# Four attention layers on one core: the second layer in steps of two units, the third layer's projections in halves

## The chip, the cores and the metric

The kernel runs on one core of a Trainium2 chip. The metric is the device time of one execution in microseconds. Before the change it is 1268.54 us, the median of three runs (1267.23 to 1269.7). The core has five engines that run beside one another, each in its own program order: PE (matrix multiply), DVE (vector), ACT (activations and copies), POOL (general) and SP (issues DMAs). They are synchronised by semaphores alone, so an instruction waits only for what its engine waits for just ahead of it.

## The reference, cut to what matters

Four layers follow one another on tokens x (4 batches of 256 tokens, 256 wide) with one context (4 x 256 x 256). The first is large (two cross attentions of 16 heads, 128 wide, and an MLP). The three others have small heads. The kernel calls them l = 1, 2, 3, and l = 1 and 2 are what the change touches:

```python
# l = 1 ("first small-head layer"): 16 heads, 16 wide, 256 context keys, mask, then an MLP
x = layer_norm(hidden, ln1_w, ln1_b)
q, k, v = x @ q_w + q_b, ctx @ k_w + k_b, ctx @ v_w + v_b
scores = where(mask, q k^T * scale, min);  out = softmax(scores) v
hidden = out @ cproj_w + cproj_b + residual
# l = 2 ("second"): queries from the latents y, keys from ctx and y together: 512 keys
h = concatenate([ctx, y], axis=1)
q, kv = y @ q_w + q_b, h @ kv_w + kv_b
attn = softmax(where(full_mask, q k^T / 16, -inf));  out = attn v @ out_w + out_b + residual
# l = 3: 32 heads, 8 wide, 8 key heads, full additive mask
```

All of it is float32. Exactness is kept by splitting operands in a high and a low part: a projection of one 128-row block is six matmuls of 256 columns (three products for each of two halves of the depth, `mm3`).

## The kernel before, in words

`class Heads` (line 1198) holds the plan of one small-head layer, and `heads_pe`, `heads_act`, `heads_dve`, `heads_pool` and `heads_sp` write it out for each engine. The work is a list of units. In layer 1 a unit is one head of one batch (64 units, 16 a batch), in layer 2 half of the queries of one head against 512 keys (128 units, 32 a batch). For each unit:

- `by_query` (L1975): scores with the queries as rows, into one of the `SB` banks; two matmuls of 256 columns (L1987) in layer 1, one of 512 (L1983) in layer 2. `maxima` on DVE reads the bank (L2233 or L2236) and so frees it.
- POOL splits the maxima of a group in high and low (L2274, L2276), PE transposes them (`turn_maxima`, L2079), ACT copies them (L2173) and POOL sends them by DMA as two more rows of the query tile Q (L2290).
- `by_key` (L1992): L steps later, the scores again with the keys as rows and the maximum and mask subtracted by the added rows (two matmuls, L2001), into one of the two `STB` banks, and ACT's exp (L2159) from there into `PT`.
- `attend` (L2056): values times `PT` for four heads at once (L2069) into bank `OB`, and ACT copies it (L2167).

A pair of units has y = 0 and y = 1: the first has its operands in partitions 0 to 63, the second in 64 to 127. The queries and the keys are 49 and 51 rows deep.

One pass of the loop `for n in range(s.steps())` is a step. WIDTH is the units of a step, LAG the steps from a unit's queries to its keys, TURN when the maxima are transposed, MEET when and in how many parts `attend` runs. Layer 1 has WIDTH 1, LAG 11, TURN 3, MEET (2, 2): a step is one unit of queries and one of keys (with the other y), written by `queries` and `keys`, and each attend is two parts in two steps. It has two `SB` banks; the transposed maxima have a bank of their own (`RB`). Layer 2 has WIDTH 2, LAG 5, TURN 1, MEET (1, 1), written by `fours`, and three `SB` banks, the third being `RB`; the maxima are transposed into the right half of `OB`.

What else is in the steps stands in tables by the step's number within a batch. IN_LAYER: the preparations for the next batch. These are the transposition of its tokens ("turn", bank PB), their high and low part ("th" on ACT, "tl" on DVE), the projections for queries, context keys, latent keys (layer 2 only, "x0", "x1", into bank MB from the second batch on) and values, each with a high part on ACT ("qh", "kh", "xh", L1602), a low part on DVE ("ql", "kl", "xl", L1641), and six DMAs from SP that spread the heads over partitions ("q_out", "k_out", "x_out", L1468). HELD gives the order in which the preparations hold bank PB. POSTS: the previous batch's output (transpose "po", divide "on", transpose "onT", split "oth" and "otl", output projection "c0", "c1", sum "y"), all in bank MB. NEXT_NORMS: the normalisation ahead of the MLP that follows. IN_MLP: the first batch's preparation, inside the MLP ahead of the layer. FC1: at which steps after the last unit the MLP's first two blocks run.

In steps with little to do PE also runs matmuls on ones whose result nobody reads (L2113, 512 columns): by `keep_busy` and `fill_step`, into `STB[1]` before the first keys, into `OB` later. In layer 1 there are 52 of them over the whole layer, in layer 2 there are 64, as counted from the tables.

Of the kernel before, what the change touches and what calls it, by code (L numbers as in the profile page):

```python
# [1123 lines left out]
def attn_end(c, w):  # L1124
# [16 lines left out]

WIDTH = {1: 1, 2: 2, 3: 2}
LAG = {1: 11, 2: 5, 3: 5}

GROUP = {1: 4, 2: 2, 3: 4}
TURN = {1: 3, 2: 1, 3: 1}

MEET = {1: (2, 2), 2: (1, 1), 3: (1, 1)}

# [15 lines left out]
              9: ["turn", "th", "tl", "res"], 10: ["q0", "q1", "qh", "ql"], 11: ["q_out"]}}  # L1165
IN_LAYER = {1: {0: ["mask", "turn", "scale"], 1: ["th", "res"], 2: ["tl", "k0"], 3: ["k1", "kh", "maskrow"],
# [9 lines left out]

HELD = {1: ("kvtq", "tkqv"), 2: ("kvtqxw", "tqkvw"), 3: ("kvtq", "tqkv")}

POSTS = {1: {2: ["po0", "on0"], 3: ["po1", "on1"], 4: ["onT", "oth"], 5: ["otl"], 6: ["c0"], 7: ["c1", "y"]},
# [6 lines left out]

NEXT_NORMS = {1: {0: [(0, "stats")], 2: [(0, "norm")], 4: [(0, "turn"), (0, "scale")], 6: [(0, "parts")],
                  8: [(1, "stats")], 10: [(1, "norm")], 12: [(1, "turn"), (1, "scale")], 14: [(1, "parts")]},
              2: {0: [(0, "stats")], 2: [(0, "norm")], 4: [(0, "turn"), (0, "scale")], 6: [(0, "parts"), (1, "stats")],
# [4 lines left out]

FC1 = {1: (2, 6), 2: (1, 3), 3: ()}


class Heads:
    def __init__(self, c, l, sl, n_x, Y, above):

        self.above = above
        self.l, self.W, self.n_x, self.Y = l, c.W[sl], n_x, Y
        self.nh, self.d, self.nkv = nh, d, nkv = {1: (16, 16, 16), 2: (16, 16, 16), 3: (32, 8, 8)}[l]
        self.nkt = nkt = 4 if l == 2 else 2
        self.NK = 128 * nkt
# [19 lines left out]
        self.SB, self.STB, self.OB, self.MB, self.RB, self.PB = c.B[1:3], c.B[3:5], c.B[0], c.B[5], c.B[6], c.B[7]  # L1225
        self.turned = self.RB[0:4 * self.G, 0:128]
        if l > 1:

            self.SB = [c.B[1], c.B[2], c.B[6]]
            self.turned = self.OB[0:4 * self.G, 256:384]  # L1230
# [53 lines left out]
    def x_bank(self, b):  # L1284
        return self.MB if b else self.PB

# [92 lines left out]
def spread_done(c, w, l):  # L1379
# [14 lines left out]
ONES_AT = {1: {0: ("q", 1, 0), 1: ("q", 1, 1), 3: ("v", 1, 0), 7: ("q", 2, 0), 8: ("q", 2, 1), 11: ("v", 2, 0)},  # L1394
           2: {1: ("q", 1, 0), 2: ("q", 1, 1), 3: ("v", 1, 0), 4: ("v", 1, 1)}, 3: {1: ("v", 1, 0)}}
# [121 lines left out]
def heads_prep_pe(c, s, b, x):  # L1517
# [27 lines left out]
    if x == "turn":  # L1545
        prep_bank_free(s, w, S, b, "t")
        if l == 1:
            w.wait_ge(S["ln_xn"], 13 + b)
            turn4(pe, ps, c.scr["xn"], c.ident).then_inc(S["h_T"])
        else:  # L1550
            w.wait_ge(S[s.n_x[0]], s.n_x[1] + b)
            turn4(pe, ps, c.X[:, 2 * b:2 * b + 2, :], c.ident).then_inc(S["h_T"])
    elif x in ("q0", "q1"):
# [18 lines left out]
    elif x in ("x0", "x1"):  # L1572
        if b:

            w.wait_ge(S["m_x"], 4 * l)
            w.wait_ge(S["lx"], b)
            if b == 3:
                w.wait_ge(S["h_y"], s.pk(0) + 1)
        else:
            prep_bank_free(s, w, S, b, "x")  # L1580
# [12 lines left out]
def heads_prep_act(c, s, b, x):  # L1593
# [25 lines left out]
    elif x == "th":  # L1619
        w.wait_ge(S["h_T"], s.pk(b) + 1)  # L1620
        tokens_free()
        act.copy(hTh, s.PB[:].rearrange("p (a b) -> p a b", a=2)).then_inc(S["h_hi"])
    elif x == "qh":
# [9 lines left out]
def heads_prep_dve(c, s, b, x):  # L1633
# [43 lines left out]
    elif x == "tl":  # L1677
        w.wait_ge(S["h_hi"], s.pk(b) + 1)
        src = c.scr["xn"][:] if l == 1 else s.PB[:].rearrange("p (a b) -> p a b", a=2)
        dve.tensor_tensor(hTl, src, f32(hTh), ALU.subtract).then_inc(S["h_lo"])  # L1680
# [279 lines left out]
def heads_pe(c, s, nxt):  # L1960
# [53 lines left out]

    def queries(n, y):

        if y == 0 and n < s.T and n % s.TB == 0:
            ready(n // s.TB)
        if y == 0 and n < 2:
            w.wait_ge(S["m_gelu"], 16 * l)  # L2020
        for k in s.in_step(n)[y:y + 1]:
            by_query(k)

    def keys(n):

        for k in s.in_step(n):
            by_key(k, 0)
            by_key(k, 1)

    def fours(n):  # L2030
# [25 lines left out]
    def attend(gi, k, n):  # L2056
# [17 lines left out]
    def turn_maxima(g, n):  # L2074
        w.wait_ge(S["t_np"], s.o["g"] + g + 1)
        w.wait_ge(S["t_rows"], s.o["g"] + g)
        if l > 1:
            w.wait_ge(S["t_os"], s.o["os"] + s.attended_by(n - 1))
        pe.transpose(s.turned, f32(s.np[:, g % 2]).rearrange("p y a q t -> p (y a q t)"), c.ident[:]  # L2079
                     ).then_inc(S["t_rT"])  # L2080

    def keep_busy(n):


        if n < s.L:
# [3 lines left out]
            return
        if l == 2:  # L2090
            return
        off, parts = MEET[l]
        g, k = divmod(n - s.L - off + 1, s.four)
        if l == 3 or n >= s.T + s.L or g > 0 and 0 < k <= parts:
            return
        w.wait_ge(S["m_x"], 4 * l)
        w.wait_ge(S["t_os"], s.o["os"] + max(0, g if k else g - 1))
        ones(s.OB, 1)

# [16 lines left out]
    for n in range(s.steps()):  # L2116
# [4 lines left out]
        if l == 3:  # L2121
            quarters(n)
        elif l == 2:
            fours(n)
        else:
            queries(n, 0)
            keys(n - s.L)
        for g in s.turns_at(n) if l == 1 else ():
            turn_maxima(g, n)
        for gi, k in s.attends_at(n):  # L2130
# [6 lines left out]
        for b, x in s.norms(n):  # L2137
            if x == "turn":
# [12 lines left out]
def heads_act(c, s, nxt):  # L2151
# [113 lines left out]
def heads_pool(c, s, nxt):  # L2265
# [227 lines left out]
```

## Time and profile before

| what | us |
|---|---|
| median of three runs | 1268.54 |
| the profiled execution's own time | 1269.28 |
| its span from first to last instruction | 1267.8 |
| PE busy | 1223.9 (97%) |
| DVE busy | 891.0 (70%) |
| ACT busy | 783.1 (62%) |
| POOL busy | 600.0 (47%) |
| layer 1, first maximum to the end of its drain | 696.24 to 798.30 |
| layer 2, likewise | 861.37 to about 1013.3 |
| layer 3's first maximum | 1073.8 |

PE's busy share is high by construction: the ends of matmuls are modelled, overlapping matmuls of a burst cover the gaps, and the matmuls on ones count as busy. How long something takes on PE is therefore read from the distance between two starts in the timeline and not from the busy column. A step's length is the distance between its first maximum and the next step's. A row of windows gives the stretch, its length, the busy time of PE, weight loads, DVE, ACT and POOL with their instructions in brackets, then PE's granted clock (1.00 is 2.4 GHz, 0.50 is 1.2 GHz), the busy share of the DMA engines and GB/s.

### The profile page before, as it was taken

What the parts mean: (1) busy time and instruction counts of PE and PEld (TensorE: products, weight loads), DVE (VectorE), ACT (ScalarE), POOL (GpSimd) and SP (SyncE); (2) the same over time, 40 slices, a digit from 0 to 9 for tenths busy, and PEclk for the clock granted to TensorE, in tenths of its full rate; (3) what the DMA queues carried; (4) which work ended last, traced back from release to release, by engine and by line L of the source; (5) the groups of instructions that cost most, each with busy time, mean ns of one, the idle gap of its engine ahead of it and who ended that gap; (6) DMA issues with size and microseconds to landing.
All of it is one profiled execution on the core that took longest, in us unless ns stands there. A gap on an engine that the chain in (4) does not pass through costs nothing. (4 is left out here: it accounts for less than half of the span.)

```text
span 1267.8 us, 27226 instructions
## 1 busy us (share of the span) xinstructions
PE 1223.9 (97%) x9982; PEld 1033.9 (82%) x9982; DVE 891.0 (70%) x2304; ACT 783.1 (62%) x1889; POOL 600.0 (47%) x966
## 2 busy tenths in 40 slices
PE   8999999999999999999989999899999889999997
PEld 7999999999999999999978565786665578666664
DVE  5887867779877777878855776536677664667764
ACT  4876666668866666667864655756665653555553
POOL 3884555558865554556841533504443331334333
PEclk9999999999999999999999999999998999999999
DMA  5441001104420100101411220122212012121100
GB/s 170 152 139 32 29 26 32 33 27 133 134 85 26 34 26 26 34 26 58 123 34 51 80 79 3 51 77 85 73 59 64 2 57 74 53 69 37 45 11 18
DMA packets 56820, 75.03 MB, mean 59 GB/s; under 512 B 11312, under 2 KB 30576, under 8 KB 56688
## 3 DMA queue, kind: packets, MB, share of 16 engines
q1 hardware_dynamic: 51568, 72.75, 18.7%
q8 instruction: 79, 1.29, 0.4%
q0 software_dynamic: 5120, 0.56, 0.3%
q14 instruction: 53, 0.43, 0.1%
HBM read 49.46 MB, written 1.05 MB: 40 GB/s over the span
## 5 line engine op out<-in xcount | busy, mean ns | idle before, releaser
L1095 POOL TENSOR_SCALAR E<-E,rl 128x256 f32<-128x256 f32 x256 | 243.6, 962 | 210.1 <-DVE rl L980 210.1
L2159 ACT ACTIVATE PT<-bank 128x512 f32<-128x512 f32 x320 | 176.5, 593 | 112.4 <-PE bank L2012 56.0
L846 ACT ACTIVATE QTh<-bank,bqs 128x256 fp32r<-128x256 f32 x128 | 60.8, 475 | 156.1 <-PE bank L127 155.9
L2242 DVE CUSTOM_DVE_ANT_0 Em<-bank,M 128x256 bf16<-128x256 f32 x256 | 95.1, 420 | 53.8 <-PE bank L1987 22.3
L856 ACT ACTIVATE E<-bank,nm 128x257 f32<-128x257 f32 x256 | 119.5, 481 | 1.2 <-DVE nm L950 1.1
L984 DVE TENSOR_TENSOR PTl<-bank,PTh 128x512 fp32r<-128x512 f32 x128 | 88.0, 687 | 27.3 <-ACT PTh L868 26.8
L2236 DVE TENSOR_REDUCE nm<-bank 128x1 f32<-128x512 f32 x128 | 83.6, 684 | 33.1 <-PE bank L1983 30.5
L2001 PE MATMUL bank<-Q,K 51*128 51x256 f32 (+1 forms) x640 | 104.1, 323 | 2.8 <-DMA Q<-rows 0.9
L957 DVE SCALAR_TENSOR_TENSOR QTl<-bank,bqs,QTh 128x256 fp32r<-128x256 f32 x128 | 61.5, 481 | 64.0 <-ACT KT L847 63.2
L868 ACT CAST PTh<-bank 128x512 fp32r<-128x512 f32 x128 | 75.2, 588 | 43.1 <-PE bank L771 43.1
L2290 POOL DMA_DIRECT2D Q<-rows x96 | 54.4, 568 | 95.5 <-ACT rows L2173 95.5
L950 DVE TENSOR_REDUCE nm<-bank 128x1 f32<-128x257 f32 x256 | 95.4, 414 | 3.4 <-PE bank L127 3.4
L2069 PE MATMUL bank<-PT,V 128*32 128x256 f32 x1280 | 87.4, 392 | 2.6 <-ACT PT L2159 2.6
L125 PE MATMUL bank<-KT,QTh 128*128 128x258 f32 x256 | 83.3, 326 | 3.4 <-issue 3.2
L2001 PEld LDWEIGHTS bank<-Q,K 51*128 51x128 f32 (+1 forms) x640 | 67.6, 187 | 20.4 <-ACT PT L2159 10.1
L771 PE MATMUL bank<-ident,E 128*128 128x128 f32 x512 | 76.7, 272 | 0.0
L990 DVE SCALAR_TENSOR_TENSOR OTl<-bank,cols,OTh 128x256 fp32r<-128x256 f32 x128 | 60.7, 474 | 18.2 <-ACT OTh L874 18.2
L126 PE MATMUL bank<-KT,QTh 128*128 128x258 f32 x256 | 73.3, 286 | 0.0
L2285 POOL DMA_DIRECT2D Q<-rows x64 | 37.7, 591 | 74.1 <-ACT rows L2173 71.2
L127 PE MATMUL bank<-KT,QTl 128*128 128x258 f32 x256 | 72.3, 282 | 0.0
L125 PE MATMUL bank<-PTh,Vh 128*128 128x256 f32 x256 | 71.8, 281 | 0.0
L127 PE MATMUL bank<-PTh,Vl 128*128 128x256 f32 x256 | 71.7, 280 | 0.0
(438 smaller groups left out, 4423.2 us busy)
## 6 DMA issues: line engine op xcount, KB each, us to landing
stage<-in_wts SPq DMA_DIRECT2D x99, 256.0 KB, 3.3
U<-in_vrows SPq DMA_DIRECT2D x64, 256.0 KB, 2.7
K<-stage SPq DMA_DIRECT2D x48, 128.0 KB
Q<-stage SPq DMA_DIRECT2D x48, 128.0 KB
K<-stage SPq DMA_DIRECT2D x48, 64.0 KB
Q<-stage SPq DMA_DIRECT2D x48, 64.0 KB
K<-xh SPq DMA_DIRECT2D x16, 128.0 KB, 2.9
Q<-rows POOLq DMA_DIRECT2D x96, 4.0 KB, 1.8
```

The source lines that it names most:

```text
L125: pe.matmul(o, wh, xh, start=first, stop=False, skip_group_check=skip)
L127: return pe.matmul(o, wl, xh, start=False, stop=last, skip_group_check=skip)
L771: m = pe.transpose(s.PTB[:, k * 256 + t * 128:k * 256 + t * 128 + 128], s.E[:, i % 3, t, k * 128:k * 128 + 128], c.ident[:])
L856: m = act.activation(s.E[:, i % 3, t, 0:257], bank[:, 0:257], ACT.Exp, bias=s.nm[:, r, t:t + 1], accum_out=s.ls[:, r, t:t + 1])
L950: dve.tensor_reduce(s.nm[:, r, t:t + 1], bank[:, 0:257], AX.X, ALU.max, negate=True).then_inc(S["dve_max"])
L984: dve.tensor_tensor(s.PTl[:], s.PTB[:].rearrange("p (a b) -> p a b", a=2), f32(s.PTh[:]), ALU.subtract).then_inc(S["dve_pt"])
L1095: m = pool.tensor_scalar(s.E[:, i % 3, t, 0:256], s.E[:, i % 3, t, 0:256], s.rl[:, r, t:t + 1], None, ALU.mult)
L2001: z = pe.matmul(s.STB[y][:, 256 * e:256 * e + 256], s.K[r][at, q // s.rp, o:o + 128], s.Q[r][at, q // s.blocks, :], start=l != 3 or e == 0 ...
L2069: z = pe.matmul(s.OB[32 * q:32 * q + 32, 0:256], s.V[b % s.NV][:, k, (4 * g + q) // s.rep, :], s.PT[(i0 + q) % s.NPT][:, k, :], start=k == ...
L2159: act.activation(s.PT[i % s.NPT][:, 2 * u:2 * u + 2, :].rearrange("p a b -> p (a b)"), s.STB[y][:], ACT.Exp).then_inc(S["t_ex"])
L2236: dve.tensor_reduce(nm[:, u:u + 1], bank[:], AX.X, ALU.max, negate=True).then_inc(S["t_mx"])
L2242: dve.tensor_tensor_reduce(out=s.Em[:, (2 * i + e) % 4], in0=bank[:, e * 256:e * 256 + 256], in1=s.M3[:, j, e, :], scale=-1.0, scalar=3.4e ...
```

## The change

Layer 1 takes layer 2's form: WIDTH 2, LAG 5, TURN 1, MEET (1, 1), `fours` in place of `queries` and `keys` (both deleted), a third `SB` bank, the maxima transposed into `OB` at the end of the step, `fill_step` in place of `keep_busy`'s later part. `fours` issues the four query matmuls of two units with y alternating. Its tables are rewritten for 8 steps a batch: whole projections (12 matmuls) in one step, the token transposition and scaling of a batch two batches ahead ("turn+", "scale+"), for the second batch in the last step of the MLP. Matmuls on ones: 30 in place of 52.

Layer 2 keeps its form. Its projections are in halves of six matmuls in steps of their own (k0 | k1, x0 | x1, q0 | q1, v0 | v1, v2 | v3) and in another order, the tokens of batches 1 to 3 are transposed into MB in place of PB, the output projection comes at table step 10 in place of 13, k is sent out before q. Matmuls on ones: 44 in place of 64.

The diff, cut to its core:

```diff
-WIDTH = {1: 1, 2: 2, 3: 2}
-LAG = {1: 11, 2: 5, 3: 5}
+WIDTH = {1: 2, 2: 2, 3: 2}
+LAG = {1: 5, 2: 5, 3: 5}
-TURN = {1: 3, 2: 1, 3: 1}
-MEET = {1: (2, 2), 2: (1, 1), 3: (1, 1)}
+TURN = {1: 1, 2: 1, 3: 1}
+MEET = {1: (1, 1), 2: (1, 1), 3: (1, 1)}
...
-              13: ["q_out", "stats+"], 14: ["norm+"]},
+              13: ["q_out", "stats+"], 14: ["norm+"], 16: ["turn+", "scale+"]},
...
-IN_LAYER = {1: {0: ["mask", "turn", "scale"], 1: ["th", "res"], 2: ["tl", "k0"], 3: ["k1", "kh", "maskrow"],
-                4: ["kl", "k_out"], 5: ["q0", "mask_out"], 6: ["q1", "qh"], 7: ["ql", "q_out"], 9: ["v0"],
-                10: ["v1", "va"], 12: ["stats+"], 14: ["norm+"]},
-            2: {0: ["mask", "v2-", "v3-", "vb-"], 2: ["turn", "th", "tl"], 3: ["res"],
-                4: ["q0", "q1", "qh", "ql", "maskrow"], 6: ["k0", "k1", "kh", "kl", "q_out"],
-                8: ["x0", "x1", "xh", "xl", "mask_out", "k_out"], 10: ["v0", "v1", "va", "x_out"]},
+IN_LAYER = {1: {0: ["mask", "k0", "k1", "th", "res", "tl", "kh", "kl"], 1: ["maskrow", "k_out"],
+                2: ["q0", "q1", "qh", "ql", "stats+"], 3: ["mask_out", "q_out"], 4: ["v0", "v1", "va", "norm+"],
+                6: ["turn+", "scale+"]},
+            2: {0: ["mask"], 2: ["turn", "th", "tl", "k0"], 3: ["k1", "kh", "kl", "res"],
+                4: ["x0", "maskrow", "k_out"], 6: ["q0"], 7: ["q1", "qh", "ql"],
+                8: ["x1", "xh", "xl", "mask_out", "q_out"], 10: ["v0", "x_out"], 11: ["v1", "va"], 14: ["v2"],
+                15: ["v3", "vb"]},
...
-HELD = {1: ("kvtq", "tkqv"), 2: ("kvtqxw", "tqkvw"), 3: ("kvtq", "tqkv")}
+HELD = {1: ("kvtq", "tkqv"), 2: ("kvtqxw", "kqvw"), 3: ("kvtq", "tqkv")}
-POSTS = {1: {2: ["po0", "on0"], 3: ["po1", "on1"], 4: ["onT", "oth"], 5: ["otl"], 6: ["c0"], 7: ["c1", "y"]},
-         2: {4: ["po0", "on0"], 6: ["po1", "on1"], 8: ["onT", "oth", "otl"], 13: ["c0", "c1", "y"]},
+POSTS = {1: {1: ["po0", "on0"], 3: ["po1", "on1"], 5: ["onT", "oth", "otl"], 7: ["c0", "c1", "y"]},
+         2: {4: ["po0", "on0"], 6: ["po1", "on1"], 8: ["onT", "oth", "otl"], 10: ["c0", "c1", "y"]},
...
-FC1 = {1: (2, 6), 2: (1, 3), 3: ()}
+FC1 = {1: (5, 6), 2: (1, 3), 3: ()}
...
+        self.SB, self.STB, self.OB, self.MB, self.RB, self.PB = [*c.B[1:3], c.B[6]], c.B[3:5], c.B[0], c.B[5], c.B[6], c.B[7]
+        self.turned = self.OB[0:4 * self.G, 256:384]
...
     if x == "turn":
-        prep_bank_free(s, w, S, b, "t")
+        if l == 2 and b:
+            w.wait_ge(S["m_x"], 4 * l)
+            w.wait_ge(S["lx"], b)
+            if b == 3:
+                w.wait_ge(S["h_y"], s.pk(0) + 1)
+        else:
+            prep_bank_free(s, w, S, b, "t")
...
-        for k in s.in_step(n):
-            by_query(k)
+        for e in (range(1) if l == 2 else range(2)):
+            for k in s.in_step(n):
+                by_query(k, (e,))
...
-        if l > 1:
-            w.wait_ge(S["t_rows"], s.o["g"] + s.turned_by(n))
+        w.wait_ge(S["t_rows"], s.o["g"] + s.turned_by(n))
...
-            ones(s.STB[1], {1: 2 if n >= 2 else 0, 2: 4, 3: 6}[l])
+            ones(s.STB[1], {1: 4, 2: 4, 3: 6}[l])
```

## Rows read from the trace of the kernel before

**Rows 1.** The page, parts 1 and 2: engines' busy time, and PE's granted clock.

```profile
PE 1223.9 (97%) x9982; PEld 1033.9 (82%) x9982; DVE 891.0 (70%) x2304; ACT 783.1 (62%) x1889; POOL 600.0 (47%) x966
PEclk9999999999999999999999999999998999999999
```

**Rows 2.** Windows: layer 1's four batches and drain; columns: length, then busy by engine.

```profile
696.24:716.90 20.66, 19.13 (x114) 10.91 (x113) 15.96 (x31) 13.46 (x22) 12.12 (x19) 1.00 0.25 82
716.90:737.01 20.11, 20.06 (x184) 12.11 (x180) 15.65 (x32) 13.29 (x30) 9.38 (x21) 1.00 0.26 84
737.01:760.90 23.89, 23.02 (x204) 14.82 (x204) 17.06 (x33) 13.72 (x31) 8.19 (x20) 1.00 0.21 69
760.90:782.06 21.16, 19.74 (x178) 10.78 (x170) 18.15 (x40) 12.87 (x28) 8.21 (x21) 1.00 0.02 4
782.06:798.30 16.24, 15.55 (x120) 9.37 (x117) 3.43 (x8) 8.66 (x17) 1.74 (x5) 1.00 0.01 2
```

**Rows 3.** PE's timeline in layer 1 (start, length, line): an attend part; transpositions.

```profile
732.36 0.38 PE L1987 MATMUL bank<-K,Q 49*128 49x256 f32 x1
...
732.79 0.64 PE L2069 MATMUL bank<-PT,V 128*32 128x256 f32 x8
733.36 0.38 PE L1987 MATMUL bank<-K,Q 49*128 49x256 f32 x1
...
737.10 0.66 PE L1738 MATMUL bank<-ident,OS 128*128 128x128 f32 x4
737.59 0.60 PE L178 MATMUL bank<-ident,xn 128*128 128x128 f32 x4
738.12 0.38 PE L1987 MATMUL bank<-K,Q 49*128 49x256 f32 x1
```

**Rows 4.** PE's timeline in layer 1 before the first keys.

```profile
706.25 0.50 PE L1987 MATMUL bank<-K,Q 49*128 49x256 f32 x2
706.68 0.60 PE L2113 MATMUL bank<-units 128*128 128x512 bf16 x2
707.22 0.50 PE L1987 MATMUL bank<-K,Q 49*128 49x256 f32 x2
```

**Rows 5.** PE's timeline in layer 2, steps 21 and 22.

```profile
903.51 0.50 PE L1983 MATMUL bank<-K,Q 49*128 49x512 f32 x2
...
904.18 1.93 PE L2069 MATMUL bank<-PT,V 128*32 128x256 f32 x32
906.05 0.51 PE L1983 MATMUL bank<-K,Q 49*128 49x512 f32 x2
...
906.72 0.38 PE L125 MATMUL bank<-CTh,W5x 128*128 128x256 f32 x1
...
908.25 0.27 PE L2079 MATMUL bank<-ident,np 128*8 128x128 f32 x1
908.45 0.50 PE L1983 MATMUL bank<-K,Q 49*128 49x512 f32 x2
```

**Rows 6.** DVE groups in layer 1's third batch (busy, mean ns, idle before).

```profile
L2233 DVE TENSOR_REDUCE nm<-bank 128x2 f32<-128x512 f32 x18 | 12.2, 687 | 5.0 <-PE bank L1987 4.8
L1641 DVE SCALAR_TENSOR_TENSOR stage<-bank,cols,stage 128x256 fp32r<-128x256 f32 x2 | 0.9, 475 | 0.0
```

**Rows 7.** Windows: layer 2's second, third and last batch.

```profile
893.19:928.39 35.20, 34.60 (x323) 22.80 (x322) 26.30 (x49) 23.17 (x53) 14.39 (x35) 1.00 0.25 74
928.39:967.84 39.45, 37.86 (x329) 25.06 (x328) 26.97 (x51) 23.34 (x52) 14.45 (x35) 0.91 0.29 90
967.84:1000.85 33.01, 30.44 (x286) 18.42 (x285) 28.97 (x63) 21.59 (x47) 13.82 (x36) 1.00 0.02 2
```

**Rows 8.** Layer 2, step 45: PE's timeline, then the windows about it.

```profile
958.79 0.79 PE L2001 MATMUL bank<-Q,K 51*128 51x256 f32 x4 [0.89 <-DMA Q<-rows]
...
958.20:965.00 6.80, 6.21 (x46) 3.48 (x47) 2.63 (x6) 2.12 (x5) 1.35 (x4) 0.50 0.11 41
956.00:958.00 2.00, 1.58 (x8) 0.75 (x8) 1.86 (x5) 1.17 (x3) 0.38 (x2) 1.00 0.95 294
```

More of the change, by code:

```diff
@@ L1185 @@
 POSTS_MLP = [["po0", "on0"], ["po1", "on1"], ["onT", "oth", "otl"], ["c0", "c1", "y"]]
-NEXT_NORMS = {1: {0: [(0, "stats")], 2: [(0, "norm")], 4: [(0, "turn"), (0, "scale")], 6: [(0, "parts")],
-                  8: [(1, "stats")], 10: [(1, "norm")], 12: [(1, "turn"), (1, "scale")], 14: [(1, "parts")]},
+NEXT_NORMS = {1: {0: [(0, "stats")], 2: [(0, "norm")], 4: [(0, "turn"), (0, "scale")], 5: [(0, "parts")],
+                  6: [(1, "stats")], 8: [(1, "norm")], 10: [(1, "turn"), (1, "scale")], 11: [(1, "parts")]},
               2: {0: [(0, "stats")], 2: [(0, "norm")], 4: [(0, "turn"), (0, "scale")], 6: [(0, "parts"), (1, "stats")],
@@ L1284, in x_bank @@
     def x_bank(self, b):
-        return self.MB if b else self.PB
+        return self.MB if b and self.l == 2 else self.PB
     def all(self, n):
@@ L1393 @@
             3: {2: ("k", 0, 0), 3: ("k", 0, 1), 4: ("v", 0, 0)}}
-ONES_AT = {1: {0: ("q", 1, 0), 1: ("q", 1, 1), 3: ("v", 1, 0), 7: ("q", 2, 0), 8: ("q", 2, 1), 11: ("v", 2, 0)},
+ONES_AT = {1: {0: ("q", 1, 0), 1: ("q", 1, 1), 2: ("v", 1, 0), 4: ("q", 2, 0), 5: ("q", 2, 1), 6: ("v", 2, 0)},
            2: {1: ("q", 1, 0), 2: ("q", 1, 1), 3: ("v", 1, 0), 4: ("v", 1, 1)}, 3: {1: ("v", 1, 0)}}
@@ L1551, in heads_prep_pe @@
             w.wait_ge(S[s.n_x[0]], s.n_x[1] + b)
-            turn4(pe, ps, c.X[:, 2 * b:2 * b + 2, :], c.ident).then_inc(S["h_T"])
+            turn4(pe, s.x_bank(b), c.X[:, 2 * b:2 * b + 2, :], c.ident).then_inc(S["h_T"])
     elif x in ("q0", "q1"):
@@ L1572, in heads_prep_pe @@
     elif x in ("x0", "x1"):
[L1573 to L1579, printed above, removed]
+        if not b:
             prep_bank_free(s, w, S, b, "x")
@@ L1621, in heads_prep_act @@
         tokens_free()
-        act.copy(hTh, s.PB[:].rearrange("p (a b) -> p a b", a=2)).then_inc(S["h_hi"])
+        act.copy(hTh, s.x_bank(b)[:].rearrange("p (a b) -> p a b", a=2)).then_inc(S["h_hi"])
     elif x == "qh":
@@ L1678, in heads_prep_dve @@
         w.wait_ge(S["h_hi"], s.pk(b) + 1)
-        src = c.scr["xn"][:] if l == 1 else s.PB[:].rearrange("p (a b) -> p a b", a=2)
+        src = c.scr["xn"][:] if l == 1 else s.x_bank(b)[:].rearrange("p (a b) -> p a b", a=2)
         dve.tensor_tensor(hTl, src, f32(hTh), ALU.subtract).then_inc(S["h_lo"])
@@ L2013, in add_mask @@
                   ).then_inc(S["t_st"])
[L2015 to L2021, printed above, removed]
-            by_query(k)
-    def keys(n):
-        for k in s.in_step(n):
-            by_key(k, 0)
-            by_key(k, 1)
     def fours(n):
@@ L2035, in fours @@
             w.wait_ge(S["m_gelu"], 16 * l)
-        for k in s.in_step(n):
-            by_query(k)
+        for e in (range(1) if l == 2 else range(2)):
+            for k in s.in_step(n):
+                by_query(k, (e,))
         for e in range(2):
@@ L2076, in turn_maxima @@
         w.wait_ge(S["t_rows"], s.o["g"] + g)
-        if l > 1:
-            w.wait_ge(S["t_os"], s.o["os"] + s.attended_by(n - 1))
+        w.wait_ge(S["t_os"], s.o["os"] + s.attended_by(n - 1))
         pe.transpose(s.turned, f32(s.np[:, g % 2]).rearrange("p y a q t -> p (y a q t)"), c.ident[:]
@@ L2087, in keep_busy @@
             w.wait_ge(S["m_x"], 4 * (l - 1) + 2)
-            ones(s.STB[1], {1: 2 if n >= 2 else 0, 2: 4, 3: 6}[l])
[L2089 to L2098, printed above, removed]
+            ones(s.STB[1], {1: 4, 2: 4, 3: 6}[l])
     def fill_step(n):
@@ L2122, in heads_pe @@
             quarters(n)
-        elif l == 2:
+        else:
             fours(n)
[L2125 to L2129, printed above, removed]
         for gi, k in s.attends_at(n):
@@ L2142, in heads_pe @@
                 mlp_turn(c, nxt, b)
-        if l == 2:
+        if l < 3:
             fill_step(n)
-        for g in s.turns_at(n) if l > 1 else ():
+        for g in s.turns_at(n):
             turn_maxima(g, n)
@@ L2179, in heads_act @@
     for n in range(s.steps()):
-        for g in s.turns_at(n - 1) if l > 1 else ():
+        for g in s.turns_at(n - 1):
             maxima_rows(g)
@@ L2202, in heads_act @@
             exps(k)
-        for g in s.turns_at(n) if l == 1 else ():
-            maxima_rows(g)
         for gi, k in s.attends_at(n):
@@ L2299, in heads_pool @@
             maxima_parts(g)
-        if n == 8 and s.NR > 2:
+        if n == 4 and s.NR > 2:
             ones_keys(c, s, 2)
```

5 lines of the change are left out of this document (removed).

## The prediction

> **What bounds the kernel now.** I read the page first: PE is busy for 97% of the span at an almost full granted clock, DVE for 70% [rows 1]. No other engine comes near, but PE's share says little, since overlapping ends and the matmuls on ones are in it. So I cut layers 1 and 2 in windows, one for each batch of units. The reader is to see in [rows 2] that layer 1 takes 20.66, 20.11, 23.89 and 21.16 us for its four batches and 16.24 us for its drain, 102.1 us in all, with DVE at 16.0, 15.7, 17.1 and 18.2 us of work in the four. Then PE's timeline, for the true price of each operation as the distance between starts. Last the groups on DVE and one stall in layer 2.
>
> Layer 1 is bound by PE, with DVE not far behind. A unit's queries and keys, four matmuls in two halves of the rows, take 732.79 - 732.36 = 0.43 us; before the first keys the queries alone, two matmuls in one half, also take 0.43 (706.25 to 706.68) [rows 3, 4]. A half of the array that stands empty saves no time. Two matmuls on ones take 0.54 (to 707.22) [rows 4]. In layer 2 two units' queries and keys together take 906.72 - 906.05 = 0.67 [rows 5], where layer 1 pays 2 x 0.43 = 0.86 for two.
>
> **Prices.** Attend: a part of layer 1 is 8 records in 0.57 (732.79 to 733.36) [rows 3], layer 2's whole one 32 records in 1.87 (904.18 to 906.05) [rows 5]; so 8 records are 0.43 and the entry 0.14, and layer 1's two parts in one step are 1.00 in place of 1.14. A projection of 12 matmuls is 1.53, the transposed maxima 0.20 [rows 5]; four output transpositions 0.49, four token ones 0.53 [rows 3]. On DVE a unit's maximum is 0.687 and a low part 2 x 0.475 = 0.95 [rows 6].
>
> **Layer 1, batch by batch.** In the new tables an even step is 0.67 + 1.53 + 0.20 = 2.40 where it carries a projection (three of four) and 0.67 + 0.53 or 0.54 + 0.20 = 1.4 otherwise. An odd step is 0.67 + 1.00 = 1.67 plus an output part.
>
> - Second batch: PE 3 x 2.40 + 1.4 + 4 x 1.67 = 15.3. DVE has the same 15.65 as now [rows 2]: 11.0 of maxima, and 4.65 that the new table puts almost wholly in odd steps. If neither engine can work ahead over a step's border, it takes 8.6 in the even steps (PE) and 5.5 + 4.65 = 10.1 in the odd (DVE): 18.7. With perfect overlap it is DVE's 15.7. Three score banks for two units a step allow half a step of working ahead, and each projection waits for the low part before it, since both use bank PB: I take 18.0, gain 2.1 (1.4 to 4.4).
> - Third batch, with outputs: PE 8.6 + 6.7 + 2 x 0.49 + 0.53 + 1.53 = 18.3, DVE 17.06 [rows 2]. The division, "otl" and "y" fall in even steps; step by step the larger of the two sums to 20.0. I take 19.5, gain 4.4 (3.9 to 5.6).
> - Last batch, no projections: PE 4 x 1.4 + 9.7 = 15.3, DVE 18.15 [rows 2], step by step 19.0. I take 18.7, gain 2.5 (2.1 to 3.0).
> - First batch: queries without keys for 5 steps, now two units in the time of one. But k0 and k1 are in step 0, so that "tl" and "kl" follow in step 1 and q0 waits for them: a chain of DVE and ACT, 16.0 to 21.6 us against 20.66. The transposition and scaling of the next batch's tokens moves into the MLP's last step, 0.5 us there. Net gain 0.5 (-1.5 to 4.1).
> - Drain, now 16.24 [rows 2]: keys alone 5 x 0.33 = 1.7 (half of 0.67), three attends 3.0, outputs 0.49 + 0.53 + 1.53, the MLP's token transposition 0.53, maxima 0.2, the MLP's two blocks 3.1 (12 matmuls of 512 columns, twice a projection): 11.1. With 1.6 of waits 12.7, gain 3.5 (1.2 to 5.1).
>
> Together 13.0 us, ends 7.1 and 22.2. 22 fewer matmuls on ones (6 us at 0.27), merged attends (16 x 0.14 = 2.2) and denser query and key groups (32 x 0.19 = 6.1) are inside this and not added.
>
> The Trainium skill speaks against the change here: "Tiling speeds up TensorE but not PSUM evacuation" (TensorEngine Tiling, Performance Considerations). By that rule the layer would run at DVE's pace; that is the first rival below.
>
> **Queues.** The maxima's DMAs come first in POOL's step, so behind the step before's "res", "maskrow" and the first split. From transposition to first use there were five unit steps of 1.3 us, now two steps of about 2.2: 6.5 us become 4.4. SP issues the same DMAs in the same order in layer 1. In layer 2 k goes out first, at table step 4, then mask and q, then x at step 10 as before; the next batch needs them at step 16. I cost that at nothing, hidden by those six steps. The transposition into MB waits for "lx" of the batch before and, in batch 3, for "y" of batch 0, issued a step and a half earlier; behind it on PE stand the next queries, so a late "y" would cost its lateness in full. "attend" now waits for ACT's copy of the maxima, which is first in ACT's step: nothing in steps with a projection ahead.
>
> **Layer 2.** A batch now pairs a step of 2.4 on PE and 1.4 on DVE with one of 1.2 on PE and 1.4 + 0.95 on DVE. Halves make it about 1.6 and 1.5 on PE, and the low part comes in a third. Step by step the larger sums to 36.6 now and 34.9 then for the third batch; measured are 35.20 for the second and 39.45 for the third, less its stall of about 4 [rows 7]. The 20 fewer matmuls on ones (5.4 us) are in that, as most of them stood beside DVE's work. I take 1.3 for each middle batch, 0.8 for the first, 0.6 for the last (PE 30.4, DVE 29.0 busy of 33.0 [rows 7], no projections): 4.0. The bounds are -1 (the output projection in a fuller step) and 9 (every matmul on ones on the path and two sums of 1.7).
>
> **What shorter steps lay bare.** In step 45 of layer 2 PE stood 0.89 for the maxima's DMA while the DMA engines were 95% busy with the MLP's weights; from then on the granted clock was 0.50 for 6.8 us, which cost 3.4: 4.3 in all [rows 8]. The weights still come at that place, so I leave it in. With less slack for that DMA in both layers, and fewer matmuls on ones, I add 1.5 us of waits and 1.0 for a possible further stretch at half clock: 2.5, from 0 to 6.
>
> **The sum.** 13.0 + 4.0 - 2.5 = 14.5 us off the profiled execution's own 1269.28 (span 1267.8 and 1.5 around it): 1254.8. The median shown is 0.74 lower: 1254.
>
> **Rivals.**
> 1. DVE sets the pace in lock-step. PE's gain in layer 1 turns into waiting for banks, and of the second to last batch only the low bounds remain, of the ramp the worst: 7.1, with nothing from layer 2 and 2.5 lost: 4.6, 1264. For it: DVE would be at 17.1 of 19.5 us in the third batch. Against: layer 2 ran at 29.0 of 33.0 without more loss [rows 7]. Chance 0.13.
> 2. The other sign: the maxima come late. The slack falls by 2.1 us; where the DMA engines are busy with the spreads (25% mean in the second batch [rows 2]) the keys wait and the clock halves, 4.3 us each as in step 45. The gain of 17 is gone with four such stalls; with six it is 26 lost: 1269 + 9 = 1278. From five on it decides. For it: step 45. Against: one such stall in the 64 steps of layer 2, which has this very slack already. Chance 0.10.
> 3. Layer 2's rearrangement brings nothing, as its DVE work is unchanged; layer 1 does its part: 1258. Chance 0.17.
> 4. Gains and stalls cancel, within 0.2% (2.5 us, what a measurement of this kernel can tell from no change): 0.05.
> My forecast, gains of 12 to 20 us, has 0.55.
>
> So faster 0.85, same 0.05, slower 0.10. The range is 1245 to 1266: down to most of both high bounds with one stall less, up to rival 1 with its term off a little. Outside lie rival 2, most of 4 and the extremes.
>
> **What would show it.** Right: a third batch of layer 1 below 20.5 us between first maxima, second near 18, a drain below 13.5; layer 2's second batch near 34 us; 30 and 44 matmuls on ones. Wrong: PE waiting for "nm" or for Q's rows in most odd steps of layer 1; a granted clock below 0.95 in layer 1's windows; layer 2's third batch still above 39 without a stall.

## The result, and the profile after

The changed kernel takes 1250.14 us, the median of four runs (1248.54 to 1250.94), against 1269.12 for the kernel before beside it (1267.23 to 1271.46): a ratio of 0.9847, interval 0.9832 to 0.9862, or 19 us less. A later comparison of the same two gave 0.9872 (0.9847 to 0.9896), 16.3 us. Predicted were 1254 and a gain of 14.5.

Parts 1 and 2 of the page after, for [rows 1]:

```profile
PE 1203.5 (96%) x9940; PEld 1029.8 (82%) x9940; DVE 888.7 (71%) x2304; ACT 779.8 (62%) x1889; POOL 598.9 (48%) x966
PEclk9999999999999999999999999999999999999999
```

The reader is to see that the page does not show where the time went: the gain of 19.4 us in the span (1267.8 to 1248.4) is a loss of 20.4 in PE's busy time, the other engines' work is the same to 4 us, and the clock's row differs by one digit (all 9 now, one 8 before). The windows show it. Layer 1's four batches, then layer 2's, of the kernel after (start and end, length, busy time of PE, weight loads, DVE, ACT and POOL, granted clock, share of the DMA engines, GB/s), for [rows 2, 7]:

```profile
696.93:718.30 21.37, 19.11 (x125) 11.89 (x125) 15.39 (x33) 12.74 (x23) 11.51 (x21) 0.86 0.25 81
718.30:737.21 18.91, 17.68 (x180) 12.30 (x178) 15.29 (x31) 12.56 (x29) 9.46 (x21) 0.98 0.28 89
737.21:756.30 19.09, 19.09 (x198) 13.75 (x194) 15.43 (x29) 13.12 (x30) 8.52 (x19) 1.00 0.27 87
756.30:774.53 18.23, 16.64 (x166) 10.16 (x162) 16.23 (x36) 12.58 (x28) 6.68 (x16) 1.00 0.02 3
774.53:851.49 76.96, 70.73 (x480) 58.82 (x481) 34.59 (x67) 42.66 (x72) 19.80 (x26) 0.98 0.16 53
851.49:882.27 30.78, 29.56 (x235) 18.93 (x233) 23.86 (x42) 21.77 (x44) 16.69 (x34) 1.00 0.29 89
882.27:914.86 32.59, 31.84 (x315) 21.91 (x312) 26.02 (x48) 23.09 (x52) 14.26 (x34) 1.00 0.29 80
914.86:947.20 32.34, 32.34 (x322) 23.27 (x321) 26.71 (x51) 23.26 (x52) 14.47 (x35) 1.00 0.36 110
947.20:981.59 34.39, 31.68 (x280) 18.23 (x279) 29.64 (x63) 21.80 (x48) 13.89 (x36) 0.95 0.02 2
```

| stretch | before | after | gain |
|---|---|---|---|
| start to layer 1's first maximum | 696.24 | 696.93 | -0.7 |
| layer 1, batch 1 | 20.66 | 21.37 | -0.7 |
| batch 2 | 20.11 | 18.91 | 1.2 |
| batch 3 | 23.89 | 19.09 | 4.8 |
| batch 4, to the end of its last maximum | 21.84 | 18.23 | 3.6 |
| drain and MLP, to layer 2's first maximum | 78.63 | 76.96 | 1.7 |
| layer 2, batch 1 | 31.82 | 30.78 | 1.0 |
| batch 2 | 35.20 | 32.59 | 2.6 |
| batch 3 | 39.45 | 32.34 | 7.1 |
| batch 4, to the end of its last maximum | 33.68 | 34.39 | -0.7 |
| from there to layer 3's first maximum | 72.25 | 72.74 | -0.5 |

Layer 3 has the same 169.6 us in both, and what follows it is equal to 0.1. The sum is 19.4. DVE's busy time in layer 1's third batch fell from 17.06 to 15.43 because some of its work falls in other windows now (29 instructions in place of 33).

PE's timeline of the kernel after shows the new form of a step at the prices of [rows 5]: queries and keys of two units in 0.68 (720.55 to 721.23), and an attend of 16 records in 1.00 (to 722.23), as worked out:

```profile
720.55 0.51 PE L1985 MATMUL bank<-K,Q 49*128 49x256 f32 x4
720.89 0.41 PE L1999 MATMUL bank<-Q,K 51*128 51x256 f32 x4
721.23 1.07 PE L2052 MATMUL bank<-PT,V 128*32 128x256 f32 x16
722.23 0.51 PE L1985 MATMUL bank<-K,Q 49*128 49x256 f32 x4
```

Two things went against the change in this execution. One is waiting; PE's waits from 696 to 790 of the kernel after (what, for whom; us in total, times, longest):

```profile
PE bank L2061 <- POOL np L2241: 2.2, 3, 1.4
PE bank L125 <- DVE hTl L418: 1.8, 1, 1.8
PE bank L1999 <- DMA Q<-rows: 1.0, 2, 0.8
```

Over both layers the waits for the maxima's DMA (the last row) are 2.4 us in 5 places; before, it was the one of [rows 8]. The other is the clock. Two windows of the kernel after, in layer 1's first batch and in its drain:

```profile
712.40:719.10 6.70, 6.46 (x39) 3.89 (x40) 4.84 (x10) 3.11 (x7) 2.30 (x7) 0.50 0.19 55
784.10:787.40 3.30, 3.30 (x20) 1.26 (x18) 0.00 (x0) 0.64 (x2) 0.00 (x0) 0.50 0.02 5
```

With two more of 3.4 us in layer 2 (at 964.9 and 992.2) that makes 17 us at half clock from 696 to the end of layer 2, against 10 before. By an estimate that takes half of each stretch as lost, that is some 8.5 us in place of 5.

### The profile page after: what moved, and what is told of

It is laid out like the page before. It is cut to its first block, busy times and chain, and to the rows that moved or that the text cites. A ratio compares the mean times of both kernels' runs of the same rounds, so it can differ in the third digit from the quotient of the medians.

```text
span 1248.4 us, 27144 instructions
## 1 busy us (share of the span) xinstructions
PE 1203.5 (96%) x9940; PEld 1029.8 (82%) x9940; DVE 888.7 (71%) x2304; ACT 779.8 (62%) x1889; POOL 598.9 (48%) x966
## 4 chain that ended last, share of the span: by engine, by line
PE 80%; DVE 7%; issue 5%; ACT 4%; POOL 2%; DMA 1%; ACTq 0%; DVEq 0%; POOLq 0%
PE bank L125 19%; PE bank L127 18%; PE bank L126 18%; PE bank L2052 5%; PE bank L771 4%; PE bank L1999 3%; PE bank L2009 3%; PE bank L1985 2%; PE bank L2010 2%; PE bank L1981 1%; ACT PT L2126 1%; DMA Q<-rows 1%; PE bank L178 1%; PE bank L713 1%; PE bank L1736 1%
## 5 line engine op out<-in xcount | busy, mean ns | idle before, releaser
L2126 ACT ACTIVATE PT<-bank 128x512 f32<-128x512 f32 x320 | 173.5, 594 | 92.6 <-PE bank L2010 56.0
L1999 PE MATMUL bank<-Q,K 51*128 51x256 f32 (+1 forms) x640 | 85.2, 315 | 4.9 <-DMA Q<-rows 2.4
L1999 PEld LDWEIGHTS bank<-Q,K 51*128 51x128 f32 (+1 forms) x640 | 60.0, 187 | 19.4 <-ACT PT L2126 8.5
```

The source lines that it names most:

```text
L1999: z = pe.matmul(s.STB[y][:, 256 * e:256 * e + 256], s.K[r][at, q // s.rp, o:o + 128], s.Q[r][at, q // s.blocks, :], start=l != 3 or e == 0 ...
L2126: act.activation(s.PT[i % s.NPT][:, 2 * u:2 * u + 2, :].rearrange("p a b -> p (a b)"), s.STB[y][:], ACT.Exp).then_inc(S["t_ex"])
```

## The experiments

"After" and "before" are the two kernels. Each ratio is to before on the same chip, with its interval. "By the ratio" means the ratio times before's median; it can differ by 1 to 2 us from the difference of the two medians.

Each execution also has its mean granted clock on record. In the 45 executions of before that stand beside the experiments it is 0.990 to 0.998, 0.9955 on average, and the time goes with it: 0.9 us more for each 0.001 less (a straight line through the 45). Multiplied by this slope, a difference of mean clocks gives an estimate of what the clock cost.

**1. Layer 1's part alone** (layer 2 with before's tables, bank and whole projections):

```diff
-            2: {0: ["mask"], 2: ["turn", "th", "tl", "k0"], 3: ["k1", "kh", "kl", "res"],
...
+            2: {0: ["mask", "v2-", "v3-", "vb-"], 2: ["turn", "th", "tl"], 3: ["res"],
+                4: ["q0", "q1", "qh", "ql", "maskrow"], 6: ["k0", "k1", "kh", "kl", "q_out"],
...
-        return self.MB if b and self.l == 2 else self.PB
+        return self.MB if b else self.PB
```

> Layer 1 in steps of two units, layer 2 as before the change. If the two parts are independent, layer 1 brings what its windows showed, 9.9 us (0.7 lost at its start, 8.9 up to the last maximum, 1.7 in the drain): ratio 0.992, some 1259 us. Theory A: the stall of step 45 in layer 2 (0.9 us of waiting, then half clock) belongs to layer 2's order of projections and DMAs, so it is here again. Rival B: it was a matter of when the layer starts, so it may be gone here too: then 4 us less, 1255.

Measured: 1255.81 us against 1267.37, ratio 0.9897 (0.9867 to 0.9927). By the ratio that is 13.1 us (9.3 to 16.9 by its interval), and 11.6 by the medians. Layer 1's terms in the forecast were 13.0, before their share of the 2.5 for shorter steps. Layer 2's tables, bank and order are now before's, and yet its third batch runs without the stall of [rows 8], in 35.45 where it took 39.45:

```profile
924.03:959.48 35.45, 34.85 (x329) 23.73 (x328) 26.96 (x51) 23.16 (x52) 14.45 (x35) 1.00 0.33 100
```

**2. Layer 2's part alone** (before, with the lines of experiment 1 the other way round):

> Layer 1 as before the change, layer 2 with halves, tokens in the output bank and the new order. Theory A: 9.6 us as in the windows (5.7 from the steps themselves, 3.9 from the stall of step 45): ratio 0.9925, 1259.5 us, and no half clock near step 45. Rival B (the stall went with the shift from layer 1): 5.7 us, ratio 0.9955, 1263.5.

Measured: 1263.72, ratio 0.9964 (0.9948 to 0.998), by the ratio 4.6 us (3.7 by the medians). With experiment 1 that is 1.03% + 0.36% = 1.39%, and the whole has 1.53% or 1.28%: the parts add up within their intervals. Layer 2's second and third batch:

```profile
894.07:927.62 33.55, 31.98 (x315) 22.03 (x312) 26.02 (x49) 23.09 (x53) 14.18 (x34) 1.00 0.27 78
927.62:961.92 34.30, 32.70 (x322) 23.18 (x321) 26.76 (x50) 23.41 (x52) 14.77 (x37) 1.00 0.34 103
```

These are 1 to 2 us above the same form in the kernel after. PE's waits in the layer account for it: here the maxima's DMA came late six times, and PE waited 4.7 us for it in place of 1.4.

```profile
PE bank L2003 <- DMA Q<-rows: 4.7, 6, 1.2
```

**3. Before, with the MLP's weights later**, so that they don't fall on step 45 of layer 2 (one wait on SP ahead of the four pieces):

```diff
+            w.wait_ge(S["t_ex"], s.o["ex"] + 86)
```

> The kernel before, with one wait added on SP: the four loads of the next MLP's weights start only when layer 2's exps of unit 85 are done, so after step 45's maxima have landed. Theory A (the weights' traffic delays the maxima's DMA in step 45, and the wait brings the half clock): PE no longer waits there, the granted clock stays 1.00 and 4 us go: ratio 0.997. Rival C (the spreads' traffic or POOL's own order delays it): the wait stays and the time is unchanged, or the weights come too late for the MLP and it is slower.

Measured: 1266.36, ratio 0.9984 (0.997 to 0.9998). The third batch is at full clock:

```profile
928.76:964.23 35.47, 34.87 (x330) 23.75 (x329) 26.97 (x51) 23.14 (x53) 14.40 (x35) 1.00 0.23 70
```

But two stretches at half clock of 3.4 us each stand later in the layer. The profile won 4 us in this batch, and the median only 2 by the ratio (1 by the difference of the medians); the mean clock is 0.996 in both. So the stall is no feature of the kernel that each execution pays; experiments 1, 2 and 7 have no such stall in step 45 either, and in 1 and 7 this layer and the place of the weights are as before. Whether the weights' traffic made that DMA late in the one profile that has the stall is therefore not shown.

**4. Layer 2's projections whole**, at the place of each second half, all else as after:

```diff
...
-                4: ["x0", "maskrow", "k_out"], 6: ["q0"], 7: ["q1", "qh", "ql"],
...
+                4: ["maskrow", "k_out"], 7: ["q0", "q1", "qh", "ql"],
...
```

> The changed kernel, but in layer 2 each projection is whole again (12 matmuls in the step of its second half: k in table step 3, q in 7, x in 8, v in 11, the latents' v in 15), everything else and the order as changed. Theory A: the halves are what layer 2's steps gain by (2.6 us in the second batch, 3 in the third): 5 to 7 us slower than the changed kernel, ratio to before 0.989 to 0.991. Rival D: it was the order and the removed matmuls on ones, then within 2 us of the changed kernel (0.985 to 0.987).

Measured: 1257.05, ratio 0.9905 (0.9877 to 0.9933), by the ratio as slow as with layer 1's part alone. Layer 2's second and third batch:

```profile
883.02:920.58 37.56, 35.09 (x321) 22.82 (x317) 26.34 (x48) 22.73 (x52) 14.41 (x35) 0.95 0.33 69
920.58:955.88 35.30, 34.30 (x331) 23.82 (x327) 27.03 (x49) 22.97 (x52) 14.42 (x35) 1.00 0.34 100
```

The second has 3.4 us at half clock in it, without which it would have about 35.9 (an estimate). These are before's lengths, with the order of the projections, the tokens' bank, the place of the output projection and the matmuls on ones as after: without the halves, layer 2's gain is gone. By the medians' intervals alone that is less sharp, since this one ends at 0.9933 and experiment 5's at 0.9896.

**5. The changed kernel again**, beside the three experiments that follow:

> The changed kernel once more, as the yardstick of this chip: 0.9847 as before. What the first runs left open: layer 1 alone gave 11.6 us and layer 2 alone 3.7, together 15.2, where the change gave 19.0. If the parts are independent, the ratio here should rather be near 0.988; if they help one another, 0.985.

Measured: 1251.79 against 1268.04, ratio 0.9872 (0.9847 to 0.9896). Its profile is another draw of the same program. Over both layers PE waited eight times for the maxima's DMA (total, times, longest), and behind the longest of these waits stands a stretch at half clock:

```profile
PE bank L1999 <- DMA Q<-rows: 4.9, 8, 1.6
```

```profile
736.38 0.50 PE L1999 MATMUL bank<-Q,K 51*128 51x256 f32 x4 [1.60 <-DMA Q<-rows]
```

```profile
737.20:740.60 3.40, 3.40 (x29) 1.90 (x17) 0.29 (x1) 1.17 (x3) 0.25 (x2) 0.50 0.00 0
```

That batch of layer 1, the second, took 21.56 here and 18.91 in the first profile. Steps in which that DMA is not late and the clock is full have the same length in both to 0.02 us. The last batch of each layer has no spreads beside it, and few such waits: in layer 2's only this profile has one, of 0.28 us. In layer 1's five of the ten profiles of the new form have one in its first two steps, 0.25 to 0.82 us (0.82 in the kernel after), and these five have its longest times, 17.7 to 18.2, where the others have 17.5.

**6. After without the matmuls on ones behind layer 1's first keys**:

```diff
-        if l < 3:
+        if l == 2:
```

> The changed kernel without the 10 filling matmuls on ones of layer 1 after its ramp (steps 5, 22, 24, 26, 30). Theory A: DVE bounds the last batch (16.2 us of work in 18.2), so the 10 stand beside DVE's work and cost nothing, and what they do is keep the clock up: same or up to 3 us slower, with further half clock in layer 1. Rival E: PE is the bound and each costs 0.27: 2.5 us faster, last batch 16 us.

Measured: 1248.43, ratio 0.9849 (0.9825 to 0.9873). Nothing lost and nothing won that can be told; the middle batches are 19.16 and 19.08 (18.91 and 19.09 in the kernel after), and the last one:

```profile
757.04:774.50 17.46, 15.85 (x160) 10.06 (x156) 16.14 (x36) 12.62 (x28) 6.66 (x16) 1.00 0.02 4
```

**7. Before without the same ones of layer 1**:

```diff
-        if l == 2:
+        if l < 3:
```

> The kernel before (layer 1 in steps of one unit) without the matmuls on ones of layer 1 after its ramp, 34 of them. This tells whether the change's gain in layer 1 is its form or its fewer matmuls on ones. Theory A (the form: a second unit in the other half of the rows, fewer changes of kind, three banks): at most a third of the 8.9 us up to the last maximum comes back, ratio 0.997 to 1.000. Rival H (PE bound and the ones on its path): 34 x 0.27 = 9 us less, ratio 0.993.

Measured: 1272.76, ratio 1.003 (1.0014 to 1.0046): slower, with 34 matmuls fewer. Its second, third and last batch in layer 1, for [rows 2]:

```profile
716.58:738.23 21.65, 20.88 (x181) 12.95 (x174) 15.64 (x32) 13.34 (x30) 9.49 (x21) 0.86 0.24 78
738.23:760.16 21.93, 20.63 (x192) 14.04 (x196) 16.90 (x33) 13.21 (x31) 7.73 (x18) 1.00 0.23 75
760.16:785.32 25.16, 22.52 (x171) 12.74 (x167) 18.85 (x40) 13.05 (x28) 8.72 (x22) 0.77 0.02 3
```

The third ran at full clock: 21.93 in place of 23.89. So the ones did cost 2.0 us of PE's path in the old form, and the new form, which has 19.09, saves the other 2.8 of that batch. In the last one the clock was half for 11.6 us and in the second for 5.9; without that they would have about 19.4 and 18.7 (estimates, half of each stretch taken off). So before's three batches, 65.8 us, would have about 60.0 without the ones at full clock, and the new form at full clock has 54.8 (experiment 11): of the gain in these batches about half comes from fewer matmuls on ones, and the rest from the form. What the ones cost, the clock took back with more. It is not only this profile: the mean clock of the twelve executions is 0.9853, against 0.9955 for before, which by the slope costs 9 us, and with the 4 us that this kernel is slower some 5 were freed.

**8. After with the four query matmuls unit by unit**, not with the halves of the array alternating:

```diff
-        for e in (range(1) if l == 2 else range(2)):
-            for k in s.in_step(n):
-                by_query(k, (e,))
+        for k in s.in_step(n):
+            by_query(k)
```

> The changed kernel with layer 1's four query matmuls in the order unit by unit (y0, y0, y1, y1) in place of alternating (y0, y1, y0, y1). Theory A: a matmul in one half of the rows costs 0.22 and one in the other half beside it nothing; if PE takes them strictly in order, the four take 0.65 in place of 0.43, 32 steps x 0.2 = up to 6 us where PE is the bound, some 2 to 3 us in all. Rival I: the halves have queues of their own, as the equal starts in the trace before suggest, and the order within a step is free: within 1 us.

Measured: 1249.48, ratio 0.9856 (0.9837 to 0.9876). Layer 1's third batch has 19.11 (19.09). PE's timeline has the four queries in 0.35 and all eight matmuls in 0.68, as after:

```profile
720.62 0.51 PE L1985 MATMUL bank<-K,Q 49*128 49x256 f32 x4
720.97 0.40 PE L1999 MATMUL bank<-Q,K 51*128 51x256 f32 x4
721.30 1.07 PE L2051 MATMUL bank<-PT,V 128*32 128x256 f32 x16
```

**9. The drain: the second normalisation a step earlier**, against the wait of 1.8 for "hTl":

```diff
-NEXT_NORMS = {1: {0: [(0, "stats")], 2: [(0, "norm")], 4: [(0, "turn"), (0, "scale")], 5: [(0, "parts")],
-                  6: [(1, "stats")], 8: [(1, "norm")], 10: [(1, "turn"), (1, "scale")], 11: [(1, "parts")]},
+NEXT_NORMS = {1: {0: [(0, "stats")], 2: [(0, "norm")], 4: [(0, "turn"), (0, "scale")], 5: [(0, "parts"), (1, "stats")],
+                  7: [(1, "norm")], 9: [(1, "turn"), (1, "scale")], 10: [(1, "parts")]},
```

> The changed kernel with the MLP's second batch ahead normalised one step earlier in layer 1's drain. Before this, PE stood 1.77 us in the drain for the tokens' low part and then ran 3.4 us at half clock (1.7 lost). Theory A: both are due to that chain, which the table put one step too late: 2 to 3.5 us faster, 1247 to 1248 (ratio 0.982 to 0.983), no wait of the first MLP block. Rival F: PE then waits for ACT's exps or the outputs instead: within 1 us.

Measured: 1249.39, ratio 0.9854 (0.9827 to 0.988). From the end of the last maximum to layer 2's first it takes 74.07 in place of 76.96:

```profile
776.07:850.14 74.07, 69.04 (x480) 58.34 (x481) 34.47 (x67) 42.55 (x72) 18.93 (x24) 1.00 0.17 55
```

The wait of 1.8 is gone, one of 0.8 for ACT's exp has come, and the half clock behind it is gone too. The intervals of the medians don't tell it from the kernel after.

**10. After with more ones in the first batch** (six in place of four a step before the first keys, and three ahead of each transposition of tokens, where PE had waited):

```diff
-            ones(s.STB[1], {1: 4, 2: 4, 3: 6}[l])
+            ones(s.STB[1], {1: 6, 2: 4, 3: 6}[l])
...
+        if l == 1 and n >= s.L and any(x == "turn" for _, x in s.preps(n)):
...
+            ones(s.OB, 3)
```

> The changed kernel with more matmuls on ones in layer 1's ramp (6 in place of 4 a step) and 3 ahead of each token transposition (steps 6, 14). Theory A: the half clock at 712 us (6.8 us long, 3.4 lost) comes from a ramp in which PE has little to do, as DVE and ACT bound it; with more it stays at 1.00 and 2 to 3 us go, ratio 0.982 to 0.983. Rival G: the ramp is bound by PE, the added 13 cost 0.27 each: 2 to 3.5 us slower, and the half clock comes all the same.

Measured: 1248.13, ratio 0.9842 (0.9817 to 0.9867). The half clock at 712 to 714 us, which all seven profiles of layer 1's new form without these ones have, is gone, and so is the wait of 0.59 for "xn". The first batch, for the 21.17 to 21.51 of the others:

```profile
698.16:719.02 20.86, 19.09 (x136) 11.63 (x136) 15.38 (x32) 12.52 (x23) 11.30 (x21) 1.00 0.26 83
```

In this profile two stretches at half clock came in the drain; from the last maximum to layer 2's first it took 78.49. The median alone doesn't tell this kernel from the kernel after; the mean clock of its executions is 0.9930, against 0.9892 for experiment 5 beside it.

**11. Both, experiments 9 and 10 together:**

> The two edits that helped, together: more matmuls on ones in layer 1's ramp and ahead of the token transpositions, and the MLP's second batch normalised a step earlier. No half clock near 712 us, no wait of 1.77 us in the drain. If they add up: 1245 to 1247, ratio 0.982.

Measured: 1245.44 (1245.1 to 1246.45) against 1268.52, ratio 0.9823 (0.9806 to 0.984), the lowest of all. It beats before beyond doubt; with the kernel after (0.9832 to 0.9862 and 0.9847 to 0.9896) its interval overlaps a little in the first comparison and not in the second. The mean clock of its executions is 0.9940, that of the kernel after 0.9905 and 0.9892, which by the slope is 3 to 4 of the 5 to 6 us between them. One stretch at half clock is left in the drain (774.6, 3.4 us). Layer 1's first three batches:

```profile
697.87:718.64 20.77, 19.08 (x136) 11.62 (x136) 15.37 (x31) 12.52 (x23) 11.21 (x21) 1.00 0.26 83
718.64:736.85 18.21, 17.52 (x183) 12.23 (x179) 15.30 (x31) 12.55 (x29) 9.56 (x22) 1.00 0.28 92
736.85:755.94 19.09, 19.09 (x198) 13.76 (x194) 15.41 (x29) 13.11 (x30) 8.46 (x19) 1.00 0.27 87
```

**12. The same with ones in the drain** (four and two more):

```diff
+        if l == 1 and n in (s.T, s.T + 2):
...
+            ones(s.OB, 4 if n == s.T else 2)
```

> The same with four matmuls on ones ahead of the last transposed maxima and two in the step after next of layer 1's drain, where PE stood 1.37 us. Theory A: half clock in layer 1's drain comes of these waits, and with them filled it stays away: 1 us below the kernel without them. Rival J: half clock there is a matter of chance from run to run: no difference, or 1 us slower for the six.

Measured: 1247.11, ratio 0.9824 (0.9804 to 0.9843). The drain's stretch is 74.06 at full clock, as in experiment 9 without these ones; the median shows no difference to experiment 11. This profile also has PE's wait of step 45 in layer 2 again, as long as in [rows 8], and at full clock:

```profile
936.94 0.51 PE L1999 MATMUL bank<-Q,K 51*128 51x256 f32 x4 [0.91 <-DMA Q<-rows]
```

The next half clock stands 26 us later, and the third batch took 34.22.

## Why the prediction was right

The forecast of 1254 held in sign and size, and its two main mechanisms (a denser layer 1, layer 2's projections in halves) are what the runs show: 14.5 us forecast, 19.0 and 16.3 measured. Layer 1 alone has 13.1 by the ratio and 11.6 by the medians (forecast 13.0, before the 2.5 for what shorter steps lay bare), layer 2 alone 4.6 and 3.7 (4.0). That the sum lies so near is in part luck: in the profile layer 1's terms bring 9.9 and layer 2's, without the stall of step 45, about 5.5, and the terms missed in both directions. By its steps:

- **Layer 1's middle and last batch** came near what was worked out. The third was put at 19.5 and has 19.08 to 19.12 in eight of ten profiles (the two others had part of a stretch at half clock in it); its PE sum, 18.3, is nearer than the lock-step of both engines, 20.0. The last was put at 18.7, counted to the start of its last maximum as in [rows 2]; counted so it has 16.8 to 17.5. Its gain of 3.6 is above the forecast's upper bound of 3.0, which took DVE's 18.15 us of work as a floor: in the new order DVE has 16.2 in that batch, since some of its work falls in other windows. The second was put at 18.0 and has 18.91, and 18.21 when the clock was full (experiment 11). That the gain comes from fewer ones, merged attends and denser groups was also right: experiment 7 gives 2.0 us of the third batch to the ones and 2.8 to the form. Of these the prices of the prediction explain 0.6 (four attend entries) and 1.5 (eight pairs at 0.19); 0.7 stays without a name.
- **DVE in lock-step** (rival 1) did not happen. DVE was busy 15.43 of 19.09 us in the third batch, and PE all of it. In the last batch DVE had 16.1 of 17.5 us. The Trainium skill says (TensorEngine Tiling (Array Packing), Performance Considerations) that emptying the banks may become the bound once TensorE is several times faster; by these numbers that did not decide in the third batch, and only the last one comes close to it.
- **The first batch** was mis-sized: +0.5 forecast, -1.4 measured with the transposition moved into the MLP (0.7 before the first maximum, 0.7 after it). A part of it is the clock: a stretch at half clock begins within the stall of 0.59 for "xn" or up to 2.4 us behind it in each of the seven profiles without the added ones, and where more ones removed both (experiments 10, 11, 12) the batch has 20.8 to 20.9. But that is before's length and not the 19.7 that the forecast needs, so at full clock about 1 us of the forecast gain is still missing. The term was mis-sized, and what holds the batch at 20.8 is not shown.
- **The drain** was mis-sized too: 3.5 forecast, 1.7 measured, and 4.6 possible (experiment 9). The waits, 1.4 for "np" and 1.8 for "hTl", are twice the 1.6 us that the estimate allowed, and behind the second the clock was half. Experiment 6, whose profile has both waits and a full clock there, took 75.44 in place of before's 78.63, a gain of 3.2.
- **Layer 2's middle batches** were put at a gain of 1.3 each. The nine profiles of the new form have 32.4 to 34.1 us in the second and 32.3 to 34.3 in the third, for 35.2 and 35.45: 1.1 to 2.8 and 1.2 to 3.1. The forecast is the low end, where the maxima's DMA is late often (experiment 2, six times); the profile after is near the high one. Experiment 4 shows that this gain needs the halves.
- **The stall of step 45** is the term on which the profiles differ most. The prediction said "the weights still come at that place, so I leave it in". Its half clock is in none of the 13 other profiles, and its wait came again only in the new form (0.91 us in experiment 12, at most 0.49 in others). The three that had layer 2 as before (experiments 1, 3 and 7) have no wait there and ran its third batch in 35.45, 35.47 and 35.48, and in two of them the weights came at their old place. So the full stall belonged to one execution, and 4.0 of the 7.1 us of layer 2's third batch are its absence. Without it the profile's gain is 15.4, near the forecast's 14.5.
- **What shorter steps lay bare**, 2.5 us, was right in kind: 1.5 more of waits for the maxima and 7 us more at half clock, which cost about 3.4. That is twice the estimate, and it is the part that differs from one execution to the next. The executions' mean clocks say the same without the profiles: 0.9905 and 0.9892 for the changed kernel against 0.9955 for before, by the slope 4 to 6 us. Rival 2 (from five such stalls on) came up to eight waits in experiment 5, but of 0.6 us on average and not 0.9, and of the eight only the longest had a half clock behind it.
- **The prediction's own signs.** The third batch of layer 1 is below 20.5, and layer 2's second is below the 34 that was named. One of its signs of being wrong did appear: a granted clock below 0.95 in layer 1's windows, 0.86 in the first batch, and the time held all the same. The drain "below 13.5" can't be read as it was meant, since in the kernel after an output projection and an MLP block of six matmuls that had stood before the last attend stand behind it.

Left open: why some waits bring a half clock and others of the same length do not. The mean clocks of the changed kernel's executions, 0.9905 and 0.9892, account for about 1 of the 2.7 us between its two comparisons; whether the rest is more than chance is not shown.

## What to carry to other kernels

A stall read in one profile is a draw from many: before it enters a sum, ask whether a program that is identical there has it in each execution, and sum against the stage's length without it. Split a long burst of matmuls over two steps where another engine empties its bank: here halves brought 1 to 3 us of a batch of 35, and moving whole bursts brought nothing. Matmuls on ones can be worth their place before a wait that comes in every execution (the first batch 20.8 in place of 21.4 here, though the kernel's median alone did not show it), and ten of them beside another engine's work cost nothing that could be told. Taken out of a full stage they free PE and may lose more to the clock.

## What the hardware showed that I had not expected

- Two matmuls of 256 columns in the two halves of the rows take 0.17 us a pair in a stream of four, and the order in which the four are issued makes no difference (experiment 8). The Trainium skill says that tiles of the array work independently (TensorEngine Tiling (Array Packing), Key Properties). This trace agrees: two in one half alone took 0.43 us [rows 4], and four over both halves 0.34.
- Single waits of 0.6 to 1.8 us, or a few close together, stood ahead of the stretches at 0.50 of the clock, and the stretches in layers 1 and 2 were 3.4, 6.8 or, once, 13.7 us long. The same wait does not always bring one: PE waits 1.19 us for "np" in step 56 of layer 2 in 13 of the 14 profiles, and in eight of them a half clock begins within 0.7 us of its end (experiment 12: 962.32 and 962.8), in five it does not (experiment 8: 966.50, at full clock behind it).
- Removing 34 matmuls that nobody reads made the kernel 0.3% slower.
- What differs between the profiles of one form is the maxima's DMA and the clock: where the DMA is on time and the clock is full, steps repeat to 0.02 us.
